# A Perceiver block on one core: inputs laid out beforehand for the engines, turns taken out, low parts shared between VectorE and GpSimd

## The reference

```python
x = x + xattn(layernorm(x), ctx, w1, b1, w2, b2)     # x 4x256x256, ctx 4x4096x256
x = x + windowed_attention(layernorm(x))             # 16 heads, window 64
x = x + mixture_of_experts(layernorm(x))             # 8 experts, top 2, inner 1024

def xattn(f, ctx, ...):
    bf = f @ w1.T + b1
    attn = softmax(bf @ ctx.T / 16)
    return concat(f, attn @ ctx) @ w2.T + b2
```

## Time and profile before

| | us |
|---|---|
| median of 3 runs | 628.12 (627.5 to 628.21) |
| span of the profiled execution, first to last instruction | 625.2 |
| around the span (median less span) | 2.9 |

### The profile page before, as it was taken

One profiled execution on the slowest core, in us unless ns is written; L12 is line 12 of the kernel. 1 busy time (PEld: TensorE's weight loads), 2 busy tenths in 40 slices (PEclk: granted clock), 3 DMA queues, 4 the chain that ended last, 5 costly groups with the idle time before them and its releaser, 6 DMA issues.

```text
span 625.2 us, 10865 instructions
## 1 busy us (share of the span) xinstructions
PE 604.4 (97%) x4049; PEld 517.9 (83%) x4049; DVE 459.0 (73%) x812; ACT 336.2 (54%) x604; POOL 267.4 (43%) x321
## 2 busy tenths in 40 slices
PE   8999999899999999999999999999999999999995
PEld 7889988898889988996767677888888888888884
DVE  4876678866977698767988868876867767676851
ACT  4547523673357523562776672666564746566550
POOL 4317920684247631695453552124242333424222
PEclk9999999999999999999999998999999999999998
DMA  8978987899959836882000395999999999999742
GB/s 297 327 303 225 274 314 198 225 277 274 327 165 305 246 74 197 212 226 68 2 2 2 127 390 199 330 332 332 356 309 359 329 352 331 346 336 336 244 151 84
DMA packets 66147, 152.89 MB, mean 245 GB/s; under 512 B 7648, under 2 KB 47968, under 8 KB 55200
## 3 DMA queue, kind: packets, MB, share of 16 engines
q1 hardware_dynamic: 61728, 146.04, 69.7%
q0 software_dynamic: 4368, 6.16, 4.7%
HBM read 121.91 MB, written 31.59 MB: 246 GB/s over the span
## 4 chain that ended last, share of the span: by engine, by line
PE 76%; DVE 9%; POOL 6%; ACT 3%; DMA 2%; issue 2%; POOLq 0%; DVEq 0%; ACTq 0%
PE psum L1720 19%; PE psum L1327 14%; PE psum L1452 13%; PE psum L1737 12%; PE psum L1492 9%; POOL wide_low L610 4%; PE psum L1402 2%; DVE head_max L991 2%; DVE region_a L996 1%; POOL wide_high L608 1%; PE psum L1368 1%; PE psum L1332 1%; PE psum L1595 1%; PE psum L1535 1%; DMA region_w<-sums_by_token,tokens 1%
## 5 line engine op out<-in xcount | busy, mean ns | idle before, releaser
L705 ACT ACTIVATE wide_high<-region_a 128x1024 fp32r<-128x1024 f32 (+1 forms) x108 | 107.7, 998 | 97.6 <-PE psum L1720 97.6
L1157 DVE TENSOR_TENSOR wide_low<-region_a,wide_high 128x1024 fp32r<-128x1024 f32 x92 | 112.1, 1221 | 57.9 <-ACT wide_high L705 57.9
L610 POOL TENSOR_TENSOR wide_low<-region_a,wide_high 128x512 fp32r<-128x512 f32 x64 | 82.5, 1291 | 18.2 <-ACT wide_high L705 14.4
L1737 PE MATMUL psum<-region_a,region_w 128*128 128x256 f32 x368 | 83.3, 379 | 0.0
L1492 PE MATMUL psum<-turned_high,wide_low 128*128 128x256 f32 x256 | 79.7, 311 | 2.4 <-DVE turned_low L1068 1.5
L1720 PE MATMUL psum<-wide_low,turned_high 128*128 128x512 f32 x184 | 78.0, 424 | 0.3 <-DVE turned_high L1259 0.2
L1737 PEld LDWEIGHTS psum<-region_a,region_w 128*128 128x128 f32 x368 | 69.7, 190 | 10.2
L1720 PE MATMUL psum<-wide_high,turned_low 128*128 128x512 f32 x184 | 72.3, 393 | 0.0
L1492 PE MATMUL psum<-turned_high,wide_high 128*128 128x256 f32 x256 | 72.3, 282 | 0.0
L1492 PE MATMUL psum<-turned_low,wide_high 128*128 128x256 f32 x256 | 72.2, 282 | 0.0
L1720 PE MATMUL psum<-wide_high,turned_high 128*128 128x512 f32 x184 | 72.1, 392 | 0.0
(11 more groups left out here) (230 smaller groups left out, 1242.2 us busy)
## 6 DMA issues: line engine op xcount, KB each, us to landing
region_a<-turned_up SPq DMA_DIRECT2D x23, 2048.0 KB, 9.4
region_a<-turned_down SPq DMA_DIRECT2D x23, 1024.0 KB, 7.2
region_a<-ctx_dram SPq DMA_DIRECT2D x16, 1024.0 KB, 9.2
turned_up<-region_w SPq DMA_DIRECT2D x64, 256.0 KB, 4.1
region_w<-L_ffn_wg_dram SPq DMA_DIRECT2D x16, 512.0 KB, 6.3
region_w<-L_ffn_wu_dram SPq DMA_DIRECT2D x16, 512.0 KB, 6.2
region_w<-L_ffn_wd_dram SPq DMA_DIRECT2D x16, 512.0 KB, 6.0
turned_down<-region_w SPq DMA_DIRECT2D x32, 256.0 KB, 4.0
```

Source lines behind the costliest of these rows:

```text
L610: nc.gpsimd.tensor_tensor(val_lo[:, g % 4], ctx_sb[n][:, g * PAIR:(g + 1) * PAIR, :], val_hi[:, g % 4].bitcast(F32), ALU.subtract).then_in ...
L705: return nc.scalar.activation(dst, src, ACT.Copy)
L1157: nc.vector.tensor_tensor(w_lo[:, k % RING], group_of(k), w_hi[:, k % RING].bitcast(F32), ALU.subtract).then_inc(low_ready, 1)
L1737: last = nc.tensor.matmul(to[:, 0:D], hidT[n][:, ic * P:(ic + 1) * P], rows, start=ic == 0, stop=ic == IC - 1)
```

## The change

`kernel()` now passes arrays in other layouts: the context by rows as before and also by columns (`ctx_cols`, so that a chunk lies as its turned blocks did), all weights turned. In the program:

- `turn_ctx`, the weight turns of `SETUP`, `turn_weights`, `store_piece` and the DRAM copies of the weights are gone. Chunks land in six buffers `raw` of 128x1024.
- The high part of a chunk is one ScalarE copy of 128x1024 from SBUF. Its low part reads `raw` and the high part, both in SBUF: on GpSimd for the chunks in `ON_POOL`, on VectorE for the others. Three buffers (`SPLIT`) hold split chunks; scores alternate between two pairs of banks.
- The low part of the values comes from GpSimd for even pairs and from VectorE for odd ones (`value_low`); `HIGH_ACT` is now 3, 7, 11, 15, and ScalarE makes these three pairs ahead.
- The output projection of batch `b` and the additions behind it move into the first chunk of batch `b + 1`. `queries(b + 1)` moves ahead of the two `turn_probs`.
- In the first batch the turn of x block 1, 2, 3 stands behind chunk 0, 2, 4.

```diff
+SETUP_AT = {0: 1, 2: 2, 4: 3}
+RAW, SPLIT, VALS = 6, 3, 6
+ON_POOL = [[2, 4, 6, 7], [2, 4, 6], [2, 4, 6], [2, 4, 6]]
+TURN_FREE = [14, 16, 12]
-HIGH_ACT = [1, 5, 9, 13]
+HIGH_ACT = [3, 7, 11, 15]
...
+        def wait_split(engine, b, ch):
+            pools = sum(len(ON_POOL[a]) for a in range(b)) + sum(h < ch for h in ON_POOL[b])
+            if ch in ON_POOL[b]:
+                engine.wait_ge(ctxT_low_pool, pools + 1)
+            else:
+                engine.wait_ge(ctxT_low_dve, b * CHUNKS + ch - pools + 1)
...
(SP)
+            def load_raw(b, ch):
+                at = b * CHUNKS + ch
+                if at >= RAW:
+                    wait_split(sp, *divmod(at - RAW, CHUNKS))
+                sp.dma_start(raw[at % RAW], ctx_cols[b, :, ch]).then_inc(raw_loaded[at % RAW], 16)
...
+            for b in range(1, BATCH):
+                for ch in range(RAW):
+                    load_raw(b, ch)
+                if b + 1 < BATCH:
                     sp.wait_ge(pv_done, b * PAIRS + FIRST)
+                    load_values(b + 1, range(4))
+                for ch in range(RAW, CHUNKS):
+                    load_raw(b, ch)
...
(GpSimd)
+                for ch in ON_POOL[b]:
+                    pool.wait_ge(ctxT_high, b * CHUNKS + ch + 1)
+                    nc.gpsimd.tensor_tensor(ctxT_lo[:, split_of(b, ch)], raw[(b * CHUNKS + ch) % RAW], ctxT_hi[:, split_of(b, ch)].bitcast(F32),
+                                            ALU.subtract).then_inc(ctxT_low_pool, 1)
+                    if b == 0:
+                        add_b2(ON_POOL[0].index(ch))
+                    if b > 0 and ch == 4:
+                        rows_normed(b - 1)
+                    if b > 0 and ch == 6:
+                        rows_biased(b - 1)
...
+                    if g not in HIGH_ACT:
+                        value_room(pool, b, g)
...
+                    if g % 2 == 0:
                         pool.wait_ge(val_high, b * highs + g + 1 - sum(h < g for h in HIGH_ACT))
...
(ScalarE)
+                        at = b * CHUNKS + ch
+                        act.wait_ge(raw_loaded[at % RAW], 16 * (at // RAW + 1))
+                        if ch >= SPLIT:
+                            act.wait_ge(scores_done, b * (CHUNKS * TPB) + (ch - SPLIT + 1) * TPB + FIRST)
+                        elif b > 0:
+                            act.wait_ge(pv_done, (b - 1) * PAIRS + TURN_FREE[ch] + FIRST)
+                        copy(ctxT_hi[:, at % SPLIT], raw[at % RAW]).then_inc(ctxT_high, 1)
...
                     for ch in range(CHUNKS):
                         ctx_out(ch)
+                        if b == 0 and ch == 0:
+                            queries_high_part(0)
...
+                        if b == 0 and ch - 1 in SETUP_AT:
+                            setup_copy(SETUP_AT[ch - 1])
...
-                        if g + 1 in HIGH_ACT and g > 0:
-                            values_high(g + 1)
+                        if g + 3 in HIGH_ACT:
+                            values_high(g + 3)
...
(VectorE)
+                        if ch + 1 < CHUNKS and ch + 1 not in ON_POOL[b]:
                             ctx_low(b, ch + 1)
...
+                        if b > 0 and ch == 0:
+                            outputs(b - 1)
+                    value_low(1)
+                    value_low(3)
...
                     for g in range(PAIRS):
                         probs_low(g)
...
-                        for _ in range(TURNS_V[min(b, 1)][g]):
-                            turn_weights(pieces)
-                            pieces += 1
+                        if g % 2 == 1 and g + 4 < PAIRS:
+                            value_low(g + 4)
...
+                    if b + 1 < BATCH:
+                        ctx_low(b + 1, 0)
...
(TensorE)
-                        if ch + 2 < CHUNKS:
-                            turn_ctx(b, ch + 2)
...
+                        if b > 0 and ch == 0:
+                            fused(b - 1)
+                        if b == 0 and ch in SETUP_AT:
+                            setup_turn(SETUP_AT[ch])
```

More of the change, by code:

```diff
@@ L116, in perceiver @@
         scores = [region_s[:, n * KEYS:(n + 1) * KEYS] for n in range(TPB)]
[L117 to L122, removed]
+        raw = [region_w[:, n * DC * BANK:(n + 1) * DC * BANK].rearrange("p (c n) -> p c n", c=DC) for n in range(RAW)]
+        xn = [scores[0][:, (BATCH + s) * BANK:(BATCH + s) * BANK + TPB * D].rearrange("p (t d) -> p t d", t=TPB) for s in range(BATCH)]
         qT_f, k_side_f, v_wide_f, sl0, sl1, sl2, sl3 = cut(region_a, [DC * TOK, SIDES * DC * TOK, BATCH * KEPT] + [HPC * P] * 4)
@@ L172, in perceiver @@
+        qwT, kwT, vwT, owT, gwT, qbc, kbc, vbc = cut(third_sb, [DC * D] * 4 + [DC * E] + [DC] * 3)
+        qwT, kwT, vwT, owT, gwT = [part.rearrange("p (c n) -> p c n", c=DC) for part in (qwT, kwT, vwT, owT, gwT)]
+        gate = sb("centred_gate", DC * E)[:, :].rearrange("p (c e) -> p c e", c=DC)
         even_share, gate_mean = sb("even_share", P), sb("gate_mean", E)
@@ L375, in store_piece @@
[L375 to L380, removed]
[L381 to L386 removed]
+                    sp.dma_start(ctx_sb[b % 2][:, t, :], src[:, t, :]).then_inc(ctx_loaded[b % 2][q], 16)
@@ L582, in _, with add_b2 @@
             pool.wait_ge(b2_loaded, 16)
-            for b in range(BATCH):
+            def add_b2(b):
                 part = xr[:, b * TPB:(b + 1) * TPB, :]
@@ L705, in copy, with setup_copy @@
                 return nc.scalar.activation(dst, src, ACT.Copy)
[L707 to L713 removed]
+            def setup_copy(b):
+                act.wait_ge(setup_turned, b + 1)
+                copy(xnT[:, :, b * NTOK:(b + 1) * NTOK], bank[6 + b % 2].rearrange("p (c n) -> p c n", c=DC)).then_inc(setup_out, 1)
             def queries_high_part(b):
@@ L769, in _ @@
                             nc.scalar.activation(act_pause[:, 1:2], zeros[:, 0:1], ACT.Exp)
-                        if b == 0:
-                            for part in SETUP_AT.get(ch - 1, []):
-                                setup_copy(part)
+                        if b == 0 and ch - 1 in SETUP_AT:
+                            setup_copy(SETUP_AT[ch - 1])
                     if b > 0:
@@ L775, in _ @@
                     probs(0, 0)
-                    values_high(HIGH_ACT[0])
                     probs(0, 1)
@@ L1425, in _ @@
             setup_turn(0)
-            setup_turn(1)
             for i in range(BATCH // 2):
@@ L1468, in _ @@
                         score(ch)
-                        if b == 0:
-                            for part in SETUP_AT.get(ch, []):
-                                setup_turn(part)
+                        if b > 0 and ch == 0:
+                            fused(b - 1)
+                        if b == 0 and ch in SETUP_AT:
+                            setup_turn(SETUP_AT[ch])
                     def turn_probs(g):
```

408 lines of the change are left out of this document (149 added, 259 removed).

## The result

The changed kernel takes **635.55 us** (median of 5 runs, 634.83 to 640.98) against 628.12 (627.46 to 628.69, 5 runs) for the kernel before: ratio 1.014, interval 1.0104 to 1.0175. It is slower, by 7.4 us, and lies within the predicted range, 5.6 us above the forecast. The profiled execution is its slowest run, 640.98 us, with a span of 639.2 us.

A forecast was written before the change was run, and what follows sets the result against it. TensorE was taken as the bound; order stalls in cross attention left batch changes of +4.5, -3.9, -2.5 and -2.7 us, span 620.6; plus 6.5 for collisions and 2.9 around the span gave 630.0 us, range 620 to 638.

The forecast's parts named there:

- slower: Sign for the whole kernel: a time over 629.4 us, given a chance of 0.51.
- rival (2): Cross attention: GpSimd wins every meeting with VectorE, collisions cost 11.9 us, time 635.4 us; chance 0.22.
- The time around the span: Whole kernel: 2.9 us added to the predicted span to give the measured time.
- First score stage: First batch: stalls of 3.4, three times 1.65, and 1.05 us; stage ends at 43.9 us against 44.9 before.
- Scores' end to the first weigh: Every batch: VectorE waits for ScalarE's split copy of values 3; 7.1 us, where the third batch took 4.6.
- Value stage: Every batch: VectorE waits for ScalarE at pairs 4, 8, 12, stalls of 1.4 us each; 33.3 us against 30.2.
- Collision (a): Chunk 3, batches after the first: VectorE and GpSimd low parts meet; 0.7 or 2.1 us, taken as 1.1 x 3.
- Collision (b): Value stages: VectorE's low parts of values 7 and 11 may wait for GpSimd; 0.4 us x 2 x 4 = 3.2.
- Weight turns at nothing: VectorE: removing 96 weight turns, 66.4 us of busy time, gains nothing by itself.
- I leave that stage and the local stage at their time: Experts' and local stages: time unchanged, since only the address order of the experts' weights alters there.

The follow-up runs named there:

- profile of 633.8: Second profiled execution of the changed kernel, run again with no edit beside its variants; span 633.8 us, series median 638.36 us, ratio 1.0169.
- a_setup: Changed kernel with the first batch's x-block turns one chunk later on TensorE and their copies two split copies later on ScalarE; 632.13 us, ratio 1.0054.
- a_both: Changed kernel with VectorE's low parts of values 3, 7, 11, 15 issued behind the probabilities' low parts of pairs 0, 4, 8, 12; 605.47 us, ratio 0.9650.
- a_late: Changed kernel with a small VectorE reduction ahead of chunk 3's low part in batches after the first, so GpSimd starts first; 641.94 us, ratio 1.025.
- b_noturn: Kernel before, with expert weights delivered already turned, so without VectorE's 96 weight turns and their loads and stores; 626.63 us, ratio 0.9985.
- a_all: The kernel of a_best2 but with 16 KB instead of 8 KB runs of the experts' up weights; 599.53 us, one run of 1152.9 us left out.
- a_best2: Changed kernel with the edits of a_both and a_setup and 8 KB runs of the up weights, second series; 598.39 us, ratio 0.9532.
- a_first: Changed kernel with only the low part of values 3 moved behind the low part of the probabilities of pair 0; 623.63 us, ratio 0.9946.
- a_order: The kernel of a_best2 with, in the first batch, chunk 4's low part on VectorE and chunk 5's on GpSimd; 599.88 us.

## Why the prediction came out as it did

The time lay in the range, and "slower" was the likeliest sign. The nearest single case was rival (2) with 635.4, but its mechanism did not occur: the agreement of that number is chance. That the forecast of 630.0 came within 5.6 us is partly luck too: its terms were off on both sides, as follows. Step by step, against the profile of 633.8 whose run took 635.50 (sum of the prediction's spans: 627.1). The time around the span was 1.7 us there, not the 2.9 of the prediction, which had set a median against the span of another run; so the time is off by 5.5 us where the span is off by 6.7:

- **First score stage: right in sum, by errors that cancelled.** Predicted stalls of 3.4 behind chunk 0, 1.65 three times and 1.05; in the first profile TensorE idled 2.88, then 0.60, 1.35, 1.31 and 0.58, 6.7 us instead of 9.4. What took the place of the rest is the clock, below: after the 2.88 the granted clock fell to 0.5, and TensorE went at half pace for some us. The end came at 44.1 and 44.7 instead of 43.9. a_setup shows the order as the cause: with the turns one chunk later on TensorE the wait of 2.9 is gone, and with the copies behind the split copies on ScalarE the waits for GpSimd fall from 3.8 to 0.8. The two moves were not run apart.
- **Scores' end to the first weigh: right.** 7.2 us, predicted 7.1; removing the wait gave 1.83 a batch, where the terms (0.72 + 0.62 + 0.62) made 1.96.
- **Value stage: right in place and cause, the stall too small.** A stall is 1.74 us by the chain (four pairs take 9.22 us) and 1.69 by its removal, predicted 1.4. The path from `weigh(2)` to `weigh(4)` is 3.37 instead of 3.27, and TensorE's restart costs 0.24 that the sum left out. Over 12 stalls it is 3.5 to 4.1 us. A stage without any stall was too small as well: the prediction's 29.1 us took 29.8 in a_both (35.2 less 5.4 up to the first `weigh`).
- **Collision (a): wrong size.** Taken at 1.1 x 3; measured 0 to 0.3 a batch, since VectorE won each time by about 0.1 us and GpSimd had slack for its 1.0. The price of losing, 2.1, was exact (a_late). Choosing a mean between two outcomes of a race gave a number that neither outcome has.
- **Collision (b): too large.** Taken at 0.4 x 8. The low parts of the values on VectorE took 678 to 1025 ns, median 691, so at most 0.35 on a few of them. This cancels only a part of what was too small above: from scores' end to the end of the value stage it is 42.1 us with the clock up, where 40.4 + 0.8 was forecast.
- **Weight turns at nothing: right** (b_noturn, 0.8 us, a bit above what the measurement can tell).
- **A step that failed: "I leave that stage and the local stage at their time".** What follows the cross attention took 8.2 us longer in the profile of 639.2, mostly by gathers, and 1.8 longer in that of 633.8, where TensorE waited only 0.4 us for one. In the first profile the chain runs three times through one, for example:

```profile
501.34 1.90 DMA sums_by_token<-region_w,tokens
503.24 10.94 DMA region_w<-normed_rows,tokens
...
514.67 2.75 PE psum L1634 x12
```

  The prediction saw that the address order changes there and gave it no price. The layout made runs of 16 KB of it. a_all against a_best2 shows the price: 3.7 us on average, 0.5 to 1.1 in three runs of five and 7 to 9 in two. With 8 or 4 KB runs the stages still took 0.3 to 1.7 us more than 338.8; for that no cause is shown.
- **A term put at nothing without a reason: the clock.** No term of the sum had it, and in the profile of 633.8 it is the largest single error, three times 1.5 us and more in the first score stage. The rows of 2 us at the start of the first value stage of the other profile, 639.2 (after the same columns as above, the clock is the third number from the end):

```profile
48.00:50.00 2.00, 0.40 (x4) 0.16 (x2) 0.15 (x1) 2.00 (x5) 1.37 (x2) 1.00 0.99 395
50.00:52.00 2.00, 0.71 (x3) 0.74 (x4) 2.00 (x4) 1.73 (x5) 0.00 (x0) 0.63 0.32 131
52.00:54.00 2.00, 2.00 (x12) 2.00 (x11) 0.34 (x1) 0.00 (x0) 0.00 (x0) 0.50 0.00 0
54.00:56.00 2.00, 2.00 (x11) 2.00 (x11) 0.23 (x1) 0.86 (x2) 0.81 (x2) 0.50 0.00 0
56.00:58.00 2.00, 2.00 (x14) 2.00 (x14) 1.25 (x3) 0.44 (x2) 1.08 (x1) 0.66 0.00 0
58.00:60.00 2.00, 2.00 (x20) 2.00 (x19) 0.69 (x1) 1.31 (x4) 0.04 (x1) 1.00 0.00 0
```

  TensorE was busy 0.40 and 0.71 us in the first two rows; from 52 it is busy throughout, but does 11 or 12 matmuls in 2 us where it does 20 at 1.00. The clock had gone to 0.50, its lower level of 1.2 GHz. It costs 1.5 us in a stage (43.6 against 42.1) and 2.8 here. In the profile of 633.8 it happened in three value stages and in the first score stage.

For the span of 633.8 the ledger against 627.1 is: first batch +1.7, second +1.3, third +1.6, fourth +0.4 (the clock's 1.5 in each of the last three; in the fourth other terms were too large), the rest +1.8: together 6.8, where 6.7 is to be explained. For 639.2 it is +3.8, -0.3, +1.5, -1.2 and +8.2, together 12.0 of 12.1.

The Trainium skill's rule that the prediction weighed ("SBUF — State Buffer", Who interferes with whom: the second to issue is fully blocked) agrees with every meeting of two-operand instructions shown above: 3.40 for 2.41 on GpSimd when VectorE is ahead, 3.23 to 3.40 for 1.22 on VectorE when GpSimd is ahead. It holds for the price. Who wins has to be read from start times a tenth of a microsecond apart; the prediction had VectorE and GpSimd meet within 0.2 us there, which was right, and put a price on the meeting that neither order has.

What stays open: why runs of 16 KB delay the gathers, and why TensorE waits for them only in some executions; why the clock falls at some of equal gaps and not at others; and whether an order of the first score stage exists without a collision, which would be worth up to the 1.8 us that TensorE waits there in a_best2.

## What to carry to other kernels

When work moves from a full engine to lists on others, the gain is decided by order, not by busy time: for each instruction in a list ask what it waits for and who needs the one queued behind it. Here two edits of order, with not one instruction fewer, and shorter runs turned 1.4% slower into 4.7% faster. A change of a data layout alters the transfers of every stage that reads it, so its run length is a term of the sum even where no instruction changes.

## What the runs showed of the hardware

- TensorE's granted clock fell to 0.50 behind the idle time before the first `weigh` of a batch, and was back only after TensorE had worked on at that pace for some us (52 to 57 in the rows above). The wait of 2.9 us there (the longest in the waits above) cost 1.5 to 2.8 more in this way, but not each time: the clock fell in 12 of the 20 value stages of the five profiles that have this wait. With the wait 1.8 us shorter it fell in none of 28 (seven profiles), although in a_first each stage still had three stalls of 1.7 us.
- A VectorE normalisation (`tensor_scalar`, 128x256, one full operand in SBUF and two of one element a partition) waited for GpSimd's whole instruction like one with two full operands: the second of a pair took 2.58 us in a_order, begun within 0.1 us of a GpSimd instruction of 2.38 us, against 0.41 for one that stands free.
- The gathers of the routed tokens land later beside weight transfers with 16 KB runs (median 7.9 to 8.7 us) than beside shorter ones (7.3 to 7.8), at the same bytes; the two groups nearly touch.
